# Routed feed-forward blocks: the router product between the last down products, the last slot rows in another PSUM bank, a root after the scatters; in the later block the selection first and two more places for the hidden layer

## The reference, cut to what matters

```python
x = x + 0.5 * ffn0(layernorm(x))      # dense part + 8 experts, top 2, RMS norms
x = x + attn0(layernorm(x))           # small linear attention, hosted inside ffn0 blocks
x = x + 0.5 * ffn0(layernorm(x))
x = x + 0.5 * ffn1(layernorm(x))      # 8 experts, relu, top 4
x = x + attn1(layernorm(x))           # 16 heads
x = x + 0.5 * ffn1(layernorm(x))

# ffn0, per token
dense = rms(gelu(d @ w_gate) * (d @ w_up) @ w_down)
probs = softmax(xr @ router_w); top_w, top_i = top_k(probs, 2)
moe   = rms(sum over the two chosen e of aff[e] * (gelu(z @ we_gate[e]) * (z @ we_up[e])) @ we_down[e])
out   = rms(dense + moe)
# ffn1, per token
h = relu(x @ w1[e].T); out = sum over the top 4 e of gs[e] * (h @ w2[e].T)
```

## Time and profile before

| | us |
|---|---|
| median of three runs | 510.31 |
| lowest, highest | 509.37, 510.66 |
| the profiled execution, whole | 510.92 |
| its span, first to last instruction | 509.0 |
| PE busy in the span | 460.3 (90%) |
| DVE, ACT, POOL busy | 363.7, 271.1, 155.8 |
| mean granted TensorE clock | 0.984 |

### The profile page before, as it was taken

The page is one execution under the profiler, slowest core; times in us unless marked ns, Lnnn a source line. Parts: engine busy times, 40 slices in busy tenths (PEclk is TensorE's granted clock), DMA queues, the critical chain, the costliest instruction groups (busy, mean ns, idle before and its releaser), DMA issues. The chain is left out here.

```text
span 509.0 us, 9619 instructions
## 1 busy us (share of the span) xinstructions
PE 460.3 (90%) x3062; PEld 395.3 (78%) x3062; DVE 363.7 (71%) x1196; ACT 271.1 (53%) x599; POOL 155.8 (31%) x221
## 2 busy tenths in 40 slices
PE   1999999989999989989999887899689989799996
PEld 1788888879887888877898776788468877678885
DVE  4668797768356877376875579798487878549685
ACT  3657643544534755444855485454546767643541
POOL 2001000331007720037500255348114333415352
PEclk9999999999999999999999998999987999999999
DMA  6333250132222343142424322582776320000001
GB/s 207 104 93 95 93 187 1 43 122 85 75 93 87 112 115 94 41 136 84 137 71 136 114 62 95 57 109 43 253 204 207 103 63 2 1 2 2 32 10 41
DMA packets 35327, 45.96 MB, mean 90 GB/s; under 512 B 4400, under 2 KB 27824, under 8 KB 35280
## 3 DMA queue, kind: packets, MB, share of 16 engines
q1 hardware_dynamic: 31920, 38.55, 26.5%
q0 software_dynamic: 2304, 6.29, 3.9%
q10 hardware_dynamic: 1056, 0.52, 0.4%
HBM read 26.47 MB, written 16.25 MB: 84 GB/s over the span
## 5 line engine op out<-in xcount | busy, mean ns | idle before, releaser
L784 PE MATMUL ps<-zh,w0u_h 128*128 128x512 f32 x160 | 65.2, 407 | 1.5 <-ACT zh L1375 1.5
L785 PE MATMUL ps<-zh,w0u_l 128*128 128x512 f32 x160 | 63.5, 397 | 0.0
L786 PE MATMUL ps<-zl,w0u_h 128*128 128x512 f32 x160 | 63.4, 396 | 0.0
L784 PE MATMUL ps<-w0d_h,ah 128*128 128x256 f32 (+1 forms) x205 | 58.5, 285 | 5.0 <-ACT tmp L1433 2.8
L2220 DVE SCALAR_TENSOR_TENSOR x<-ps,aff,x 128x256 f32<-128x256 f32 x128 | 53.0, 476 | 9.8 <-PE ps L786 8.0
L786 PE MATMUL ps<-w0d_l,ah 128*128 128x256 f32 (+1 forms) x205 | 57.2, 279 | 0.0
L785 PE MATMUL ps<-w0d_h,al 128*128 128x256 f32 (+1 forms) x205 | 57.1, 279 | 0.0
L684 POOL TENSOR_TENSOR al<-act,ah 128x512 fp32r<-128x512 f32 x29 | 37.4, 1290 | 47.8 <-ACT ah L1538 44.7
L2303 DVE CUSTOM_DVE_ANT_0 ps<-ps,bias 128x256 f32<-128x256 f32 (+1 forms) x128 | 42.6, 386 | 9.9 <-PE ps L1215 9.2
L784 PEld LDWEIGHTS ps<-w0d_h,ah 128*128 128x128 f32 x205 | 38.5, 188 | 8.3 <-issue 6.2
L699 POOL TENSOR_SCALAR_AFFINE_SELECT pbt<-pbt 128x256 f32<-128x256 f32 x64 | 25.7, 407 | 61.4 <-ACT pbt L1669 61.1
(11 more groups left out here) (232 smaller groups left out, 1353.5 us busy)
## 6 DMA issues: line engine op xcount, KB each, us to landing
stage<-in_w_dram SPq DMA_DIRECT2D x16, 384.0 KB, 3.1
stage<-z_rows SPq DMA_DIRECT2D x21, 256.0 KB, 3.0
y_rows<-tmp SPq DMA_DIRECT2D x21, 256.0 KB, 2.1
qs<-split_out SPq DMA_DIRECT2D x24, 128.0 KB, 2.7
ks<-split_out SPq DMA_DIRECT2D x48, 64.0 KB, 2.5
stage<-in_w_dram SPq DMA_DIRECT2D x8, 256.0 KB, 3.1
z_rows<-tmp SPq DMA_DIRECT2D x1, 1920.0 KB, 8.1
ks<-pad SPq DMA_DIRECT2D x6, 256.0 KB, 9.4
```

Source lines behind the costliest of these rows:

```text
L784: pe.matmul(o, lh, rh, start=start, stop=False, **kw)
L785: pe.matmul(o, ll, rh, start=False, stop=False, **kw)
L786: return pe.matmul(o, lh, rl, start=False, stop=stop, **kw)
```

## The change

- `routed_start`: between the last two down products of the block before, PE now makes the router product; behind them it turns the logits at once, into bank 3 instead of 6. ACT copies `z_hi` ahead of the last `act_hi`, DVE `z_lo` ahead of the last `act_lo`, and DVE's selection follows directly. `ranks` keeps its place and takes over the waits for bank 7.
- The first slot rows are turned behind `down0` of unit 5's slot instead of ahead of it.
- The last slot unit (13) writes its down product to bank 2 (`y_bank`); PE makes the first half of unit 14 before the down products of units 12 and 13. The wait for all of `y_s` now stands ahead of the first half of unit 15.
- POOL: `moe_rms(0)` behind all scatters of block 1. DVE: `moe_norm(0)` one unit later.
- Later block: the logits and the selection come first on DVE, `exps` right behind `dense_squares` on ACT, the expert weights ahead of the first `hidden_lo`; up products go over three banks at first; units 6 and 7 have places of their own (`qh`, `ql`) and wait for no down product; `sum_squares` stands ahead of `hidden(3)`; PE makes up products 6 and 7 ahead of `down1(3)` and `down1(4)`; on DVE all four `acc1` stand behind the layer norm's statistics.

```diff
+        def y_bank(n):
+            return 2 if n % U0 == LAST - 1 else 3
...
-            return n % 2 if first_later(n) else n % 3
+            if first_later(n) and n >= 3:
+                return (n + 1) % 2
+            return n % 3
+
+        def hidden_parts(n):
+            if first_later(n) and n >= 6:
+                return qh[:, n - 6, :], ql[:, n - 6, :]
+            slot = (U0 * f0 + n) % NA
+            return ah[:, slot, :], al[:, slot, :]
...
                             for t in range(BT):
-                                if fb == 1 and t == BT - 2:
-                                    moe_rms(0)
                                 scatter(fb, t)
-                            if fb > 1:
-                                moe_rms(fb - 1)
+                            moe_rms(fb - 1)
...
+            def routed_start(st, b):
+                n = units(st, b, "ffn0")
+                which, bank = (0, 2) if st.kind == "ffn0" else (1, 3)
+                down0(n - LAG)
+                split_ready(norm(st, b))
+                pe.wait_ge(prod_s, n)
+                logits_t(which, bank, False)
+                down0(n - 1)
+                logits(3, routed[st.kind, st.k + b])
...
                     elif v == LAST:
-                        down0(n - LAG)
                         turn_act(n - 1)
                         ups(n, 0)
+                        down0(n - LAG)
                         down0(n - 1)
                         ups(n, 1)
                     else:
+                        if v == LAST + 1:
+                            pe.wait_ge(y_s, PAIRS0 * fb)
                         ups(n, 0)
...
-                        if v == DENSE - 1:
-                            turn_rows(n + 1)
                         if v == LAG + 1:
                             down0(n - LAG - 1)
                         if LAG < v < DENSE:
                             down0(n - LAG)
+                        if v == DENSE - 1:
+                            turn_rows(n + 1)
...
                         if first_later(n):
-                            if c > LAG:
+                            if LAG < c < 6:
                                 down1(n - LAG - 1)
+                            if c == 7:
+                                down1(3)
+                                down1(4)
...
             def first_block(st):
                 last, n = f0 - 1, routed["ffn1", 0]
+                z_lo(st.p)
                 left_lo(st, 0)
-                z_lo(st.p)
+                take_logits(n, 3)
+                shift_logits(n, 4)
                 for t in range(2):
                     combine(last, t)
                     moe_weigh(last, (t,))
-                take_logits(n, 3)
-                shift_logits(n, 4)
+                expert_weights(n, "ffn1", 0)
                 hidden_lo(0)
...
                 hidden_lo(1)
+                moe_norm(last)
+                sum_weigh(last)
                 hidden_lo(2)
-                moe_norm(last)
-                expert_weights(n, "ffn1", 0)
-                acc1(0)
-                sum_weigh(last)
                 finish0(last, 1)
                 prepare(st.p + 1, 0)
-                for c in (1, 2, 3):
+                for c in range(4):
                     acc1(c)
```

85 lines of the change are left out of this document (38 added, 47 removed).

## The result

The changed kernel takes 504.04 us in the median (501.7 to 505.53), the kernel before, run beside it, 509.85 us: a recorded ratio of 0.987 (that of the two medians is 0.989), 95% interval 0.9835 to 0.9906. The forecast was 501.5, range 498.0 to 505.8. Of the profiled executions the one of before took 510.92 us (span 509.0), the one of after 502.75 us (span 500.8): 8.2 us less, where the sum of the prediction had 8.8. By the medians it is 5.8: the four executions of after took 501.70, 502.75, 505.34 and 505.53 us, and the profiled one is of the quicker pair.

A forecast was written before the change was run, and what follows sets the result against it. PE was taken as the bound, busy 460.3 of 509.0 us, so only gaps or its clock could give time. Terms 0 + 3.4 + 1.4 + 4.0 = 8.8 us off 510.92 gave 502.1, 501.5 for the median; range 498.0 to 505.8.

The forecast's parts named there:

- cover fails: Rival, later block: ACT or POOL 2 us late ahead of `hidden(3)`, block gives 1.5, not 4.0; 505 us, chance 0.22.
- Block starts: Starts of three blocks, router product first: loss of 0.5 in block 1, gains of 0.2 in blocks 2 and 3; sum 0.
- Slot rows: PE's waits for the first slot rows from DRAM shrink in three blocks: 2.0, 1.0 and 0.4 us, sum 3.4.
- a down product of 1.45 stands ahead of the turn and covers 1.29 and 0.6 whole: Blocks 2 and 3: the down product moved ahead of the slot rows' turn hides their waits of 1.29 and 0.6 us.
- The root: Block 1, POOL: with the root no longer ahead of the fifth scatter, the slot rows land 2.3 us earlier.
- Last slot rows: Block ends: waits of 0.88 to 1.03 us for bank 3 go; 0.9 in block 1, 0.5 in block 2, sum 1.4.
- Later block: Later block: earlier selection and statistics shorten the block and the low parts behind it; 4.0 us, block 3's share included.
- The same queue in the new order: Later block, DVE: the queue of 24.8 us starts at 293.3, loses 0.75 of gaps, gains 0.4, ends at 317.3.
- The clock: Stage behind and attention: PE's clock dips may fall otherwise, 1 us either way.
- Slower: the clock: Rival, later block and attention's start: spread waits drop PE's clock, six more stretches give 511.7 us; slower by over 0.3%, chance 0.05.
- The signs: PE's list: no `stage` wait over 0.3, none for `tmp`; later block: selection near 288.5, `acc1` end 312.5, `transposes` 311.3.
- The table load: ACT, later block: a skill rule would add a 1.38 us drain, giving 2.6 instead of 4.0; the trace before showed none.

The follow-up runs named there:

- e5_zlo_first: Changed kernel, but in block 1 DVE makes `z_lo` ahead of the accumulation `left_acc(3)`; 505.65 us, ratio 0.9904.
- e9_three_orders: Changed kernel with slot rows turned ahead of two down products, hidden tile 3's low part on DVE, block 1's low parts ahead of both accumulations; 503.07 us, ratio 0.9864.
- e2_turn_first: Changed kernel, but the first slot rows are turned ahead of the two down products again; 502.82 us, ratio 0.9867.
- e1_root_between: Changed kernel, but block 1's root on POOL stands ahead of the last two scatters again; 504.99 us, ratio 0.9898.
- e10_ranks_earlier: The kernel of `e9_three_orders` with `ranks` ahead of unit 1's first product instead of behind it; 501.55 us, ratio 0.9833.
- e3_one_bank: Changed kernel with all slot rows in bank 3 again, the last units' order and PE's wait for `y_s` as before; 507.12 us, ratio 0.9926.
- e4_pool_after_x: Changed kernel, but POOL's subtraction for hidden tile 3's low part waits for `finish0`; 505.60 us, ratio 0.9905.
- e8_lo3_on_dve: Changed kernel with hidden tile 3's low part moved from POOL to DVE, behind tile 2's; 502.35 us, ratio 0.9846.
- e6b_later_again: Second run, on another chip, of the changed sorted blocks with the later block as before the change; 504.67 us, ratio 0.9901.

## Why the prediction was right, and where it was not

- *The number.* The median lies in the range, but 2.5 us above the forecast, and in the interval of the rival "cover fails" (503.5 to 507, chance 0.22), not in the forecast's own (499.5 to 503.5, 0.52). By the medians the change gives 5.8 of the 8.8 us. The 8.2 of the two profiled executions are in part luck, as the last points say.
- *Bound.* That only gaps count held: PE's busy time is the same within 0.4 us.
- *Block starts, 0.* From `transposes` to `ranks`: 10.47, 10.63, 10.64 before, 11.02, 10.39, 10.39 after. Loss of 0.55, gains of 0.24 and 0.25, against 0.5, 0.2 and 0.2. The wait for `zl` in block 1 was 1.03 us, forecast "near 1". `e5_zlo_first` and `e9_three_orders` show it can't be ordered away on DVE.
- *Slot rows, 3.4.* What block 1 and 2 gained over the forecast's other two terms is 2.4 + 0.55 - 0.9 = 2.05 and 2.3 - 0.24 - 1.1 = 1.0, as forecast (2.0, 1.0); for block 3 the rows give 0.2 where 0.4 was forecast. The size was right and **the cause half wrong**: the step "a down product of 1.45 stands ahead of the turn and covers 1.29 and 0.6 whole". `e2_turn_first` shows that without it only 0.63 of wait comes back in one block (0.79 and 0.62 in `e9_three_orders`), and that it costs 0.6 in block 1. What the prediction did not count is that the routing in blocks 2 and 3 itself comes earlier: the last scatter ends 0.3 to 0.9 us sooner, part of which may be chance. The root was right: 1.0 us in `e1_root_between`.
- *Last slot rows, 1.4.* The store of block 2 was quick (2.56 us where before's took 3.98), so 1.1 instead of 0.5 there: luck, which the prediction had named. The wait for `y_s` that the prediction placed in block 2 came in block 3 (0.39) and, in other executions, in block 1 (0.96, 1.15) or in block 2 (1.12, `e10_ranks_earlier`): the mechanism is the one named, the store's landing, and it moves from block to block. `e3_one_bank` shows the term.
- *Later block, 4.0.* Here **the sum failed**. PE's four waits were forecast at 0.4, 1.2, 0.9 and 1.6 us and came at 0.44, 0.85, 0.61 and 1.57. The step that failed is "The same queue in the new order": DVE's durations were taken over from before, where POOL stood idle beside `finish0`, and POOL's root at 1.01. In the new order they overlap and cost 0.7 + 1.0. Shown by `e4_pool_after_x` and `e8_lo3_on_dve` for the 1.0; the 0.7 of the root is read from the rows alone. The term also has a slip: the queue is said to gain a gap of 0.4, which is in the 311.0 of the statistics and not in the 317.3 of its end, so the 4.0 is about 0.4 too high by its own numbers. And a wait of PE for the first `acc1`, which now stands behind the statistics, is missing from the list: 1.07 ahead of `down1(3)`. That of `down1(5)` for the last one came at 0.81, where the prediction's own times (317.3 against 316.1 and 0.85) give 0.35. The base was unlucky too: `e6b_later_again`, with the old order, needs 1.7 us less than before for the two stretches, because in before's trace the last store of block 3 landed late (0.9) and the clock fell (0.7). Against it the new orders lost 1.0 us up to attention, where 3.5 were forecast.
- *The clock.* The prediction gave it 1 us either way and a rival on the slow side. It came out 1.5 on the good side, in the attention (81.8 us in before, 80.3 in after). That is luck: in eight of the ten other traces of the new order the attention takes 80.9 to 82.0. So the total of 8.2 against 8.8 owes its closeness to errors that cancel: 2.8 too much in the later block, against 1.5 too little for the clock, 0.6 for block 2 and 0.4 from the stretch ahead of block 1, where nothing was changed.
- *The rivals.* "Cover fails" (505) has the right end for several of the executions, in the main by another mechanism: not ACT's queue ahead of `hidden(3)`, whose wait came as forecast (1.57), but DVE and POOL. What it said of the cover did come: PE's 0.6 us of lead were gone at the `transposes`. "Slower: the clock" found nothing: in none of the eleven traces of the new order does the clock fall in the later block.
- *The signs.* The waits for `stage` are gone, one for `tmp` is left (0.39). The selection starts at 288.11 (288.5), but the four `acc1` end at 314.65 (312.5) and the `transposes` start at 312.89 (311.3), 1.6 us and more too late.
- *The table load* in its new place: 289.43 to 290.71, the exponentials start at 290.72, again without a drain that the trace would show.

## What to carry to other kernels

When an order is costed by moving a queue with its old durations, list what the neighbour engine does at the new times: here one of DVE's instructions and two of POOL's grew by 1.7 us together beside work that had stood elsewhere. Moving the neighbour's work behind may only lengthen its queue (0 gained); giving it to the engine that idles just there gained the full 1.06. And a reason for a gain should be undone by itself before it is kept: the down products ahead of the turn looked like 1.9 us of cover; with the root moved they cost 0.6 us in block 1 and nothing that the time could tell. Last, a base read from one execution carries that execution's luck: a store that landed 2.3 us late and a fallen clock stood in the rows of the later block, and 1.7 us of "gain" were only their absence.
